# A graph-attention walk taken in double pairs, four of eight pairs read back from DRAM, and a count fill that signals every fourth product

## What is computed

```
x = x + gat(layernorm(x), src, dst)      # attention over edges, 4 heads
x = x + ffn0(layernorm(x))               # 8 experts, top 1
x = x + gcn2(layernorm(x), src, dst)     # two graph convolutions with batchnorm
x = x + ffn1(layernorm(x))               # 8 experts, top 2
# gat:
e     = leaky_relu(el[src] + er[dst], 0.2)
alpha = softmax of e over the edges of one dst
rst   = segment_sum(feat[src] * alpha, dst);  return h + elu(rst + bias)
```

## Time and profile before

| | us |
|---|---|
| median of 3 runs (7734.77 to 7762.5) | 7741.1 |
| the profiled execution's own time | 7729.86 |
| its span, first to last instruction | 7728.1 |

### The profile page before, as it was taken

One profiled execution on the slowest core, in us unless ns is written; L12 is line 12 of the kernel. 1 busy time (PEld: TensorE's weight loads), 2 busy tenths in 40 slices (PEclk: granted clock), 3 DMA queues, 4 the chain that ended last, 5 costly groups with the idle time before them and its releaser, 6 DMA issues. The chain is left out here.

```text
span 7728.1 us, 130980 instructions
## 1 busy us (share of the span) xinstructions
PE 5449.5 (71%) x37484; PEld 4407.3 (57%) x37485; DVE 3508.0 (45%) x10470; ACT 1732.1 (22%) x4193; POOL 2142.1 (28%) x2057
## 2 busy tenths in 40 slices
PE   2411115655577777777764995999969999549998
PEld 1200003333355555555543994888858888539997
DVE  5411117866666666666675555111161121532222
ACT  0200004666622222222222333000020000133332
POOL 2477770000055555555542220000000000052221
PEclk8655557877788888788875998999989999759999
DMA  3476661222244444444434662444402222336665
GB/s 119 121 212 195 193 202 58 92 86 98 101 116 116 118 116 116 116 115 116 117 91 135 177 177 75 157 152 157 158 26 102 96 95 92 121 136 181 183 180 169
DMA packets 448603, 1001.55 MB, mean 130 GB/s; under 512 B 56758, under 2 KB 314157, under 8 KB 428812
## 3 DMA queue, kind: packets, MB, share of 16 engines
q1 hardware_dynamic: 329116, 650.63, 26.1%
q0 software_dynamic: 112144, 268.88, 13.4%
q10 hardware_dynamic: 7200, 80.28, 2.5%
HBM read 713.64 MB, written 295.09 MB: 131 GB/s over the span
## 5 line engine op out<-in xcount | busy, mean ns | idle before, releaser
L671 POOL DMA_INDIRECT arena<-table,arena x1664 | 1674.6, 1006 | 2056.5 <-DVE arena L760 1623.9
L1249 PE MATMUL banks<-arena 128*128 128x256 bf16 x14700 | 1625.5, 273 | 25.5 <-DMA arena<-counts 25.5
L1249 PEld LDWEIGHTS banks<-arena 128*128 128x128 f16 x14700 | 1440.4, 98 | 206.7 <-DMA arena<-counts 26.3
L607 PE MATMUL banks<-arena 128*128 128x392 bf16 x2368 | 651.9, 436 | 1108.8 <-issue 718.8
L831 PE MATMUL banks<-arena 128*128 128x261 f32 x3328 | 1188.5, 489 | 162.0 <-DVE arena L760 81.3
L607 PEld LDWEIGHTS banks<-arena 128*128 128x128 bf16 x2368 | 350.1, 152 | 1410.1 <-issue 1373.4
L831 PEld LDWEIGHTS banks<-arena 128*128 128x128 f32 x3328 | 697.4, 233 | 276.4 <-DVE arena L760 93.6
L1868 POOL DMA_INDIRECT expert_in<-arena,slot x147 | 148.3, 1009 | 2306.2 <-DVEq L1809 2263.3
L1303 DVE TENSOR_TENSOR rings<-rings,banks 128x256 f32<-128x256 f32 x98 | 41.3, 421 | 1347.4 <-PE banks L1241 1347.4
L585 DVE TENSOR_TENSOR arena<-arena 128x1024 bf16<-128x1024 f16 x296 | 203.9, 689 | 988.5 <-remote 487.4
L2084 PEld LDWEIGHTS banks<-yt_ring,arena 128*128 128x128 f32 x5184 | 607.7, 193 | 15.4 <-DVE yt_ring L1973 4.1
(11 more groups left out here) (325 smaller groups left out, 5096.9 us busy)
## 6 DMA issues: line engine op xcount, KB each, us to landing
arena<-counts SPq DMA_DIRECT2D x100, 1568.0 KB, 6.6
arena<-in_L_ffn_W SPq DMA_DIRECT2D x114, 1024.0 KB, 5.2
edge_rows<-arena SPq DMA_DIRECT2D x312, 264.0 KB
arena<-edge_rows SPq DMA_DIRECT2D x312, 264.0 KB
counts<-arena ACTq DMA_DIRECT2D x50, 1568.0 KB, 5.1
arena<-in_L_ffn_w SPq DMA_DIRECT2D x64, 1024.0 KB
expert_in<-arena SPq DMA_DIRECT2D x25, 2028.0 KB
arena<-table,arena POOLq DMA_INDIRECT x1664
```

What stands on the lines that cost most here:

```text
L607: pe.matmul(psum_all[:, bass.ds(at_[p % 16], KEYS)], oh_b[:, p // LB % (OR // LB), :, p % LB], oh_k[:, p // KB % (OR // KB), :, p % KB], s ...
L671: pool.indirect_dma_start(out=got[:, u, j, :], out_offset=None, in_=table0, in_offset=bass.IndirectOffsetOnAxis(ap=src_sb[:, 2 * pair + j: ...
L1249: last = pe.matmul(psum[u][:, 0:D], a_ring[:, u, a, :], parts[:, a, k, :], start=(a == 0 and k == 0), stop=(a == NT - 1 and k == 2))
```

## The change

Two pairs are now one **double pair** of 4 x 128 edges, with UQ = 4 places to a step and 416 in all. Each of DVE's and ACT's operations on a pair is done once for both (`collect` stays one for each pair), PE issues the products of both behind each other with one signal at the end, the gathers are four in a row with one wait ahead of them, and SP's transfers are twice as large. The memory is the same, so messages, turned one-hots and PSUM results now have two places, the one-hots and `got` four. Kept places are (0, 1, 4, 5), the double pairs 0 and 2 of each step: 416 pairs are stored and read back, 416 gathered in the walk. The order in a slot is new on PE and DVE. In the fill, `done` is signalled by every fourth product, `hot` once for 8; the number for `zeroed` is packed into the loaded bank number, and the units' ends are rounded up to whole groups of four.

```
-KEPT = (0, 3, 6)
+KEPT = (0, 1, 4, 5)
...
+UQ = UN // 2
...
                         for p in range(BP):
                             if p % LB == 0:
                                 if p >= OR:
-                                    dve.wait_ge(done, p - OR + LB)
+                                    dve.wait_ge(done, (p - OR + LB) // PG)
...
-                                if p % PG == PG - KB:
+                                if p % LB == LB - KB:
                                     last.then_inc(hot, 1)
...
                             if p % PG == 0:
-                                pe.wait_ge(zeroed, need[p % 16 // PG])
-                                pe.wait_ge(hot, p // PG + 1)
-                            pe.matmul(psum_all[:, bass.ds(at_[p % 16], KEYS)], oh_b[:, p // LB % (OR // LB), :, p % LB],
-                                      oh_k[:, p // KB % (OR // KB), :, p % KB],
-                                      start=False, stop=False, skip_group_check=True).then_inc(done, 1)
+                                need = pe.snap(bank & 511)
+                                bank = pe.snap(bank & (7 * 512))
+                                pe.wait_ge(zeroed, need)
+                                if p % LB == 0:
+                                    pe.wait_ge(hot, p // LB + 1)
...
+                            if p % PG == PG - 1:
+                                last.then_inc(done, 1)
...
+                        for n in range(NKEPT // 2):
+                            i, q = divmod(n, UQ)
+                            wait(pool, s_st[q], 16 * i)
+                            fetch(pool, q, 2 * n)
...
+                                three, two = later_(i, q, 3), later_(i, q, 2)
+                                if three:
+                                    copy_onehot(*three)
+                                if two:
+                                    weights(*two)
...
+                            for q in range(UQ):
+
+                                two, one = later_(i, q, 2), later_(i, q, 1)
                                 if one:
                                     messages(*one)
                                 if two:
+                                    score_sum(*two)
                                     score_max(*two)
-                                collect(i, u, tile(u))
+                                collect(i, q, 0, tile(2 * q))
                                 if two:
                                     score_clamp(*two)
+                                collect(i, q, 1, tile(2 * q + 1))
                                 if not final(i):
-                                    make_onehot(i + 1, u)
+                                    make_onehot(i + 1, q)
...
-                        def turn(i, u):
-                            pe.wait_ge(s_oh, UN * i + u + 1)
+                        def turn(i, q):
+                            pe.wait_ge(s_oh, UQ * i + q + 1)
...
-                            wait(pe, s_acc, n - RB + 1)
+                            wait(pe, s_acc, 2 * (n - 1))
...
-                                add_up(i, u)
-                                if u + 4 < UN or not final(i):
-                                    turn(i + (u + 4) // UN, (u + 4) % UN)
-                                if u + 3 < UN or not final(i):
-                                    spread(i + (u + 3) // UN, (u + 3) % UN, tile(u))
+                                three, two = later_(i, q, 3), later_(i, q, 2)
+                                if three:
+                                    turn(*three)
+                                if two:
+                                    spread(*two, lambda v: tile(2 * q + v))
+                                add_up(i, q)
```

More of the change, by code:

```diff
@@ L46 @@
 STEPS = PAIRS // UN
-KEPT = (0, 3, 6)
+KEPT = (0, 1, 4, 5)
 LIVE = tuple(u for u in range(UN) if u not in KEPT)
 NKEPT = len(KEPT) * STEPS
+UQ = UN // 2
+KEPT_Q = tuple(u // 2 for u in KEPT[::2])
+LIVE_Q = tuple(u // 2 for u in LIVE[::2])
 assert NKEPT % UN == 0
+assert all(a % 2 == 0 and b == a + 1 for k in (KEPT, LIVE) for a, b in zip(k[::2], k[1::2]))
 PCH = math.ceil(PAIRS / P)
@@ L667, in tiles_of, with fetch @@
                     return lambda u: eng.snap((words[u // 4] // (1 << (6 * (u % 4)))) % 64)
-                def fetch(pool, u, pair):
-                        for j in range(2):
-                            pool.indirect_dma_start(out=got[:, u, j, :], out_offset=None, in_=table0,
+                def fetch(pool, q, pair):
+                        for j in range(4):
+                            pool.indirect_dma_start(out=got2[:, q, j, :], out_offset=None, in_=table0,
                                                     in_offset=bass.IndirectOffsetOnAxis(
@@ L785, in body @@
                             tile = tiles_of(dve, i, mybir.EngineType.DVE, tpack)
-                            for u in range(UN):
-                                two = (u + 2 < UN or not final(i)) and (i + (u + 2) // UN, (u + 2) % UN)
-                                one = (u + 1 < UN or not final(i)) and (i + (u + 1) // UN, (u + 1) % UN)
-                                if two:
-                                    score_sum(*two)
+                            for q in range(UQ):
+                                two, one = later_(i, q, 2), later_(i, q, 1)
                                 if one:
@@ L810, in turn, with spread @@
                                                  start=True, stop=True)
                             last.then_inc(s_t, 1)
-                        def spread(i, u, t):
-                            pe.wait_ge(s_ht, UN * i + u + 1)
-                            wait(pe, s_z, UN * i + u - 1)
-                            for j in range(2):
-                                for k in range(3):
-                                    last = pe.matmul(banks_e[u][:, j, :], onehot_t[:, u % RB, j, :],
-                                                     arena16[:, bass.ds(t * 24 + (parts_at + 8 * k), 8)],
-                                                     start=(k == 0), stop=(k == 2))
+                        def spread(i, q, tile):
+                            pe.wait_ge(s_ht, UQ * i + q + 1)
+                            wait(pe, s_z, UQ * i + q - 1)
+                            for v in range(2):
+                                t = tile(v)
+                                for j in range(2):
+                                    for k in range(3):
+                                        last = pe.matmul(banks_e[q % 2][:, 2 * v + j, :], turned[:, q % 2, 2 * v + j, :],
+                                                         arena16[:, bass.ds(t * 24 + (parts_at + 8 * k), 8)],
+                                                         start=(k == 0), stop=(k == 2))
@@ L982, in _ @@
                         link(dve.tensor_copy(order[:, u, :], own_[:, k, :]))
[L983 removed]
+                for table, lo in ((tpack, 0), (tpack4, 4)):
                     four = trow2[:, lo:lo + PAIRS].rearrange("p (s u) -> p u s", u=4)
```

208 lines of the change are left out of this document (110 added, 98 removed).

## The result

The changed kernel takes 8870.4 us (median of 4 runs, 8867.25 to 8875.01), the kernel before 7744.35 us (4 runs, 7734.77 to 7762.5): a ratio of 1.1451, interval 1.1436 to 1.1467. The forecast was 8515 us, its range 7780 to 9050. The profiled execution took 8875.01 us, its span is 8873.2 us, the mean granted clock 0.792.

The account below looks back on a forecast made before the run. The fill beside gathers was taken as bound by the number of PE's signals, the changed walk by a closed PE-DVE loop. 7730 - 205 (fill) + 980 (walk) = 8505, 8515 us as median; range 7780 to 9050, own range 8220 to 8810.

Parts of the forecast that it names:

- Kept gathers: Before the walk: 832 kept gathers for 624, ending at 1449 to 1500 us instead of 1166.
- gathers over 2 us each: Beside the fill: sign that the forecast is wrong; DVE stopping POOL would give a gather each 2.4 us.
- The fill: Count fill: 2 signals for 8 products instead of 8, ending at 1875 us instead of 2081, -205 us.
- the fill gains nothing: Rival on the fill: between +140 and +50 us, taken as +90, giving 8800 us; chance 0.10.
- a signal as long as a fetch: Fill beside gathers: a signal takes a doubled fetch's 5.6 us, fill ending at 2224, +140 us; rival's shared chance 0.10.
- DVE in POOL's way: Fill: DVE's blocks stop POOL 2.7 of every 5.6 us, kept gathers until 2140, +50 us; rival's shared chance 0.10.
- Fewer operations on DVE: Walk: seven operations for twelve, DVE's own work for two pairs from 3.2 us to about 2.7.
- The closed loop: Walk: new order puts one-hot, turn, spread, sums and collects in series; a slot of 6.55 us against 4.64.
- term 5: Walk: PE's sums signalled late beside gathers in every second slot, adding 0.45 us a slot.
- Late signals: Walk: every second slot's add_up late by 0.9 us beside gathers, 0.45 us a slot, making 7.0 us.
- the loop at full clock: Rival on the walk: slots of 5.4 us, no signal late, +314 us, giving 7850 us; chance 0.20.
- at half clock: Rival on the walk: loop slots of 7.7 us plus 0.5 for late signals, +1479 us, giving 9015 us; chance 0.12.

Follow-up runs that it names:

- e2: Kernel before with only the change's fill (a signal for every fourth product, hot for 8): 6419.36 us against 6464.05, ratio 0.9934.
- e6: Changed kernel with PE issuing add_up (the sums) ahead of turn and spread in each slot: 7810.65 us against 7738.08 for the kernel before, ratio 1.0096.
- e5: Changed kernel run once more, unedited: 8867.33 us against 7738.08 for the kernel before, ratio 1.1463.
- e7: Changed kernel without gathers in the walk, SP reading all four double places from stored rows: 8860.5 us, one run.
- e8: Kernel before without gathers in the walk, SP reading all places from stored rows: 7178.33 us against 7738.08, one run.
- e3: Kernel before with fill products of 196 columns instead of 392, every signal kept: 6415.2 us against 6464.05, one run.

## Why the prediction was right or wrong

**Kept gathers: right, at the lower bound.** 1456 us, where 1449 was the sum and 50 us stood for DVE's blocks. The blocks come no more often than before, 188 operations of DVE in 826 us against 185, so there was little to hold POOL up. The rival by which they would (gathers over 2 us each) did not come: 1.37; and in e2, where DVE is busy nearly all the time, it is 1.46.

**The fill: wrong in sign, by 442 us.** The step that failed is "So beside gathers the fill is bound by the number of PE's signals". The rows gave 23.1 us for a block of eight products, and eight signals went with eight products; I took the signals for the cause. With two signals a block it is 22.4 us, and they come 11.2 us apart: the price is 2.8 us for each product. What made signals look guilty is that the earlier trace rows show the products ending after 2.83 us; the ends of matmuls in the record are modelled, and what DVE waited for came far behind such an end. The working also set DVE's start at 744.92 against the wrong block: the one done at 726.53 is the last, and DVE waits for the one before it, in the record done at 704.84 (723.70 - 18.86), 40.1 us earlier and not 18.4. That PE stands a whole block behind its record is what eight products of 2.8 us each look like, one after the other. The arithmetic that does hold: kept gathers 290 us longer; 104 products made meanwhile that then need not be made at 0.44 us (1954 in 861 us), -46; and 0.441 against 0.445 us for each of the others, -8. That gives the +236 us. The rival "the fill gains nothing", at 8800 us, was nearest to the result by its number, and that is luck: its two mechanisms, a signal as long as a fetch and DVE in POOL's way, are both not what happened. In it the fill's end was 50 to 140 us late; it is 236.

**Fewer operations on DVE: right that it would not show, too large in size.** It was to bring DVE's own work on two pairs from 3.2 us to about 2.7. DVE is busy 1326 us in the walk before, 3.19 for two pairs, and 1273 now, 3.06 a slot; in e6 it is 1268. So 0.13 us is saved, not 0.5. The term had no part in the sum.

**The closed loop: right, and shown (e6 against e5, and e7).** The forecast had PE idle 1.9 us ahead of the turn; it is 2.1. It had 4.65 us for PE's part as the mean of 3.5 and 5.8; it is 4.72. It had DVE idle 2 us or more at the first collect; it is 3.07. Opening the loop by one moved call gives 1056 us back. A slot was put at 6.55 us before term 5 and is 6.79 (2824 / 416), 0.24 more: 0.21 on DVE's side, where PE is idle 2.11 us for a forecast of 1.9, and 0.03 in the rest. The granted clock was guessed at half the time on each level, 0.75. The profiled execution shows that, but e5 shows 0.63 for the same walk of 2824 us, and the other three executions behind the result have a mean clock of 0.75 where the profiled one has 0.79, at the same time within 0.1%. So the length of PE's part is confirmed, and that it comes of half the time on each level is not.

**Late signals: wrong.** 0.45 us a slot was added and e7 shows zero. In the timeline of the slot above, a collect starts 0.27 us after the end of the sums. The 0.45 too much and the 0.24 too little leave the walk 78 us shorter than forecast.

**The sum.** The fill's 442 us less the walk's 78 are 364 us; 8505 + 364 = 8869 for the profiled execution, which took 8875. Nothing outside the two terms is left to explain, and the two errors cancel only in small part. The time lies 60 us above the forecast's own range (8220 to 8810) and inside the one for 8 times in 10, which was wide enough to hold the fill's error: the sign and most of the size are the loop's, but that the fill's wrong sign did not leave the range is luck. The rivals with the loop at full clock (5.4 us a slot) and at half clock (7.7) bracket what came.

**Open** stays why on one kind of chip a product beside gathers takes 2.8 us. The stretch after the last gather is free of it, and POOL's gathers, their DMAs and the stores all end together there. For the walk e8 narrows it: PE's results are late beside gathers at 115 GB/s and not beside SP's reads at 158.

## What to carry to other kernels

When a ring is made of fewer, larger pieces, write down for each wait which slot makes what it waits for and which queue stands behind it: a turn that used to run four pairs ahead here became the head of the queue in front of the sums, and one call's place was worth 1056 of 1126 us. Merge pieces, then put the work that others wait for first. A count of events read off one stretch does not tell which of several things that always come together costs the time; here products and signals came one to one, so that the price had to be bounded by the case that it belongs to the products (nothing gained), not only by other prices of a signal. And look for a change's sign on more than one chip where a stretch is unlike its neighbours: the same walk by double pairs with the sums first gained 164 us on one and lost some 280 us on the other.

## What the runs showed of the hardware

Two kinds of chip run the same kernel in 7740 and 6460 us. The difference lies in the stretches with gathers: products of the fill beside them 2.79 us against 0.34 each, the walk 1932 against some 1427 us. With its gathers taken out (e8) the walk of the slower kind takes 1384 us, so the difference comes with the gathers; by what way was not shown. The changed kernel itself never met the faster kind.

Where products come fast, 592 `done` for 2368, with the `hot` halved and one table less to load, gave 45 us (e2). The Trainium skill, "TensorE: Matmul & The Clock Gate", section "The cost: per-tile semaphore tail", has 26.3 ns for an increment; by that figure, an estimate, 1776 fewer are 47 us. e2 has that size, but does not show that it is the signals' price: half the columns with every signal kept gave 49 us (e3). On the other kind of chip the same edit gave nothing beside gathers (296 products in 826 us both times) and 8 us behind them (0.441 for 0.445 us a product), where by that figure, an estimate, 1466 fewer signals would be 39.
